# Routed experts of a two-layer Flamingo block: which operand is stationary, where the down weights come from, and how far ahead rows are gathered

## The chip, the cores and the metric

The program runs on one core of a Trainium2 chip. The time is the device time of one execution in microseconds (us), of which the median of several runs is taken. The engines are TensorE (PE, its weight loads PEld), VectorE (DVE), ScalarE (ACT), GpSimd (POOL) and SyncE (SP), which issues most transfers.

## What is computed

`x` is 8 tiles of 128 tokens by 256. Layer 0 adds a gated recurrent cross attention and then a gated mixture of experts; layer 1 adds a gated attention over the context and a gated feed-forward part with block-quantised weights and activations. The change touches the mixture of experts alone:

```python
idx, share = top 4 of 64 experts for each token      # router_w, softmax
for each expert e among them:
    h = silu(row @ wg[e]) * (row @ wu[e])            # row 256, wg and wu (64, 256, 64)
    y = y + share[e] * (h @ wd[e])                   # wd (64, 64, 256)
y = y + two shared experts(row)
x = x + tanh(g_ffn[0]) * y
```

## The kernel before, in words

All numbers are float32. The 1024 x 4 picks of tokens are sorted into 128 blocks of 64 rows (`S = 64`, `NBLK`). The first 64 blocks belong to fixed experts, block e to expert e (`NSTAT`); picks that do not fit there go to the other 64 blocks, whose expert is known only at run time, from the table `eid_row`. Four blocks are a "pair" (two tiles of 128 rows, each two blocks, `Q = 2`); there are `NP = 32` pairs, of which `NPS = 16` are fixed (0 to 15) and 16 are "chosen" (16 to 31). All up and gate weights (`moe_up`) and all down weights (`moe_dn`) are brought into SBUF.

Each pair goes through these steps, and each engine walks the pairs in one loop with an order written out by hand; semaphores tie the loops together:

- POOL gathers the pair's 256 rows from `h1_dram` by two indirect DMAs (L542) into `xg`, which has four buffers. Between them it rescales a chunk of the quantised weights of the last layer (L534).
- TensorE turns the rows (four transposes through the helper `turn`, L1214) into banks 0 and 1, and ScalarE copies them into `xgT` (L740). `xgT` has room for the two blocks of a tile apart, so that each can stand in a tile that is zero elsewhere; two memsets of VectorE (`clear`, L1001) provide the zeros.
- Up products: rows are stationary, weights move. In `up_fixed` (L1371) the two blocks of a tile use the left and right 64 columns of the array. In `up_chosen` (L1380) a tile with one block and zeros is stationary over all 128 columns, and the weights are picked by a register (`experts_of`, L337).
- ScalarE takes the silu of the gate half (L733), VectorE multiplies it by the up half into `hb` (L1078).
- Hidden turns: TensorE turns `hb` (two transposes), ScalarE copies the result into `hbT` (L754 for fixed, L756 and L757 for chosen pairs).
- Down products: four products of 64x64 stationary by 256 moving columns (L1398 fixed, L1401 chosen). For chosen pairs SP fetches the four experts' down weights a second time from DRAM into `dnS` (L399), two pairs ahead.
- ScalarE copies the result into `ysb` (L746), and SP stores it to `ys_dram` (L418).

In TensorE's loop step k does: up products of pair k, row turns of pair k + 1, down products of pair k - 2, hidden turns of pair k - 1. VectorE also quantises the last layer's weights in halves (`weight_half`), one half for each fixed pair and two for each chosen pair. Behind the routed stage TensorE turns these weights (`mx_turns`, L1214, with fill products `keep_warm`, L1444, between), POOL gathers the experts' results for each token (L566), and VectorE adds them up and normalises (L1095, L1152); then the attention of layer 1 begins.

Before the stage, at 84 us, stand the router's products (L1309, 64 moving columns) and those of the shared experts (L1237 and L1224, 256 moving columns).

## Time and profile before

| what | value |
|---|---|
| median of 3 runs | 512.68 us (511.4 to 513.83) |
| time of the profiled execution | 514.03 us |
| its span, first to last instruction | 512.3 us |
| mean granted TensorE clock | 0.92 of full speed |
| TensorE busy | 406.5 us, 79% |
| VectorE, GpSimd, ScalarE busy | 351.4, 247.5, 181.4 us |
| routed stage, first up product to first turn of the last layer's weights | 158.7 to 290.4 us |
| first up product of a chosen pair | 214.6 us |

The profile is one execution as the hardware profiler recorded it. Times within it are us from the start of the span. A line such as L1380 is a line of the kernel's source. The span is shorter than the time of the same execution, because the latter also has what lies before the first and behind the last instruction.

### The profile page before, as it was taken

The page shows a single profiled execution, that of the slowest core. Times are in us where ns is not written, and L with a number is a line of the kernel's source. Part 1 is how long each engine was busy: PE and PEld are TensorE (multiplying, and loading weights), DVE is VectorE, ACT ScalarE, POOL GpSimd, SP SyncE. Part 2 cuts the span into 40 slices and gives each one's busy share as a digit, 9 for nine tenths or more (in the row PEclk, how much of TensorE's full clock was granted, in tenths as well). Part 3 has the DMA queues.
Part 4 walks back from the last instruction along what each step waited for, and adds up shares of the span by engine and source line. Part 5 has one row for each costly group of instructions (what it writes and reads, how often), then busy time and mean ns, then how long its engine had stood idle before and what let it go on. Part 6 is the DMA issues. An engine that isn't in the chain of part 4 may idle for free.

```text
span 512.3 us, 8514 instructions
## 1 busy us (share of the span) xinstructions
PE 406.5 (79%) x2839; PEld 289.6 (57%) x2839; DVE 351.4 (69%) x840; ACT 181.4 (35%) x416; POOL 247.5 (48%) x347
## 2 busy tenths in 40 slices
PE   0476788778677899999699678768887899988884
PEld 0265666666446566677477456556665455555543
DVE  0568886656986455589577326857857699999992
ACT  0353465445301454444244242325354122222210
POOL 2356565423227577777441265866212245555451
PEclk9987798879959899999899699979997999999998
DMA  7999961112923597668954342433110000000000
GB/s 222 266 216 271 242 237 52 52 52 59 170 41 100 130 297 224 173 173 181 161 150 142 118 137 80 146 87 118 57 42 1 0 1 12 10 10 12 11 10 22
DMA packets 72314, 57.42 MB, mean 112 GB/s; under 512 B 38864, under 2 KB 64592, under 8 KB 72272
## 3 DMA queue, kind: packets, MB, share of 16 engines
q1 hardware_dynamic: 60880, 37.23, 27.9%
q0 software_dynamic: 4608, 12.59, 10.8%
q10 hardware_dynamic: 6784, 7.05, 4.1%
q8 instruction: 24, 0.39, 0.3%
q14 instruction: 18, 0.15, 0.1%
HBM read 42.18 MB, written 14.68 MB: 111 GB/s over the span
## 4 chain that ended last, share of the span: by engine, by line
PE 47%; issue 16%; DVE 15%; POOL 10%; ACT 3%; DMA 3%; ACTq 3%; another core or an unknown queue 2%; POOLq 0%; DVEq 0%
PE psum L1214 9%; PE psum L1380 6%; PE psum L1401 4%; PE psum L1237 3%; PE psum L1398 3%; POOL arena_dn L628 3%; PE psum L1371 3%; POOL mx_w L631 2%; PE psum L1224 2%; PE psum L1283 2%; DMA bias_bc<-_xattn_norm_k_img_w_dram 2%; PE psum L1229 2%; PE psum L1281 2%; PE psum L1470 2%
## 5 line engine op out<-in xcount | busy, mean ns | idle before, releaser
L542 POOL DMA_INDIRECT shared<-h_dram,tok_u x64 | 66.9, 1046 | 49.9 <-PE psum L1214 22.3
L1501 PE MATMUL psum<-arena_dn 128*128 128x512 f32 x128 | 57.1, 598 | 3.2 <-ACT arena_dn L785 3.2
L628 POOL TENSOR_TENSOR arena_dn<-arena_dn 128x512 f32<-128x512 f32 x16 | 20.3, 1271 | 45.6 <-DVE arena_dn L1047 45.6
L1501 PEld LDWEIGHTS psum<-arena_dn 128*128 128x128 f32 x128 | 23.7, 190 | 31.2 <-issue 26.3
L566 POOL DMA_INDIRECT arena_up<-ys_dram,slot_u x32 | 31.4, 981 | 14.1 <-issue 14.1
L1078 DVE TENSOR_TENSOR h1T<-psum,h1T 128x128 f32<-128x128 f32 x32 | 9.3, 292 | 40.0 <-ACT h1T L733 37.4
L1214 PE MATMUL psum<-ident,mx_w 128*128 128x128 f32 x128 | 23.3, 312 | 16.2 <-POOL mx_w L631 8.9
L1214 PE MATMUL psum<-ident,arena_dn 128*128 128x128 f32 x96 | 18.3, 310 | 21.8 <-DVE arena_dn L878 19.3
L1214 PE MATMUL psum<-ident,arena_up 128*128 128x128 f32 x144 | 25.0, 292 | 12.4 <-DVE arena_up L1105 2.9
L1214 PEld LDWEIGHTS psum<-ident,mx_w 128*128 128x128 f32 x128 | 16.8, 158 | 27.1 <-POOL mx_w L631 10.9
L1596 PE MATMUL psum<-arena_dn,mx_w 128*128 128x256 f32 x128 | 30.1, 390 | 0.4 <-ACT mx_w L795 0.3
L1214 PEld LDWEIGHTS psum<-ident,arena_dn 128*128 128x128 f32 x96 | 13.9, 163 | 26.4 <-issue 16.3
L1214 PEld LDWEIGHTS psum<-ident,arena_up 128*128 128x128 f32 x144 | 17.0, 147 | 20.2 <-DVE arena_up L1169 4.8
L1095 DVE SCALAR_TENSOR_TENSOR x_res<-arena_up,combs,x_res 128x256 f32<-128x256 f32 x32 | 16.5, 516 | 15.9 <-DMA arena_up<-ys_dram,slot_u 15.1
L746 ACT COPY stage<-psum 128x512 f32<-128x512 f32 x32 | 18.9, 591 | 24.0 <-PE psum L1401 14.9
L1401 PE MATMUL psum<-h1T 64*64 64x256 f32 x128 | 19.1, 419 | 10.3 <-issue 10.3
L733 ACT ACTIVATE h1T<-psum 128x128 f32<-128x128 f32 x32 | 8.9, 278 | 50.6 <-PE psum L1380 21.3
L1596 PEld LDWEIGHTS psum<-arena_dn,mx_w 128*128 128x128 f32 x128 | 24.5, 197 | 4.0 <-issue 0.8
L472 POOL TENSOR_SCALAR small<-mv 128x1 f32<-128x1 f32 (+2 forms) x26 | 6.1, 234 | 37.9 <-DVE mv L896 12.3
L790 ACT ACTIVATE arena_dn<-psum 128x512 f32<-128x512 f32 x16 | 9.6, 598 | 39.4 <-PE psum L1501 39.4
L475 POOL TENSOR_TENSOR rstd<-small,mhalf 128x1 f32<-128x1 f32 (+2 forms) x26 | 22.1, 850 | 2.2
L534 POOL TENSOR_TENSOR mx_w<-mx_w,wac 128x256 f32<-128x256 f32 x24 | 15.1, 627 | 13.2 <-DVE mx_w L1072 12.8
(226 smaller groups left out, 1065.4 us busy)
## 6 DMA issues: line engine op xcount, KB each, us to landing
ys_dram<-stage SPq DMA_DIRECT2D x32, 256.0 KB
arena_up<-in_L_ffn_wg_dram SPq DMA_DIRECT2D x8, 512.0 KB, 8.3
arena_up<-in_L_ffn_wu_dram SPq DMA_DIRECT2D x8, 512.0 KB, 7.4
h1T<-in_L_ffn_wd_dram SPq DMA_DIRECT2D x64, 64.0 KB
arena_dn<-in_L_ffn_wd_dram SPq DMA_DIRECT2D x3, 1024.0 KB, 11.5
va_dram<-stage ACTq DMA_DIRECT2D x8, 256.0 KB, 3.7
kT_dram<-stage ACTq DMA_DIRECT2D x8, 256.0 KB, 4.6
arena_up<-kT_dram SPq DMA_DIRECT2D x8, 256.0 KB, 2.7
```

Of the source, the lines that this page charges most:

```text
L475: pool.tensor_tensor(dst, temp, mhalf[:, 0:dst.shape[1]], ALU.pow).then_inc(sem(done), 1)
L542: pool.indirect_dma_start(out=xg[n % 4][:, b, :], out_offset=None, in_=h1_dram[:, :], in_offset=bass.IndirectOffsetOnAxis(ap=tok_u[:, 2 * ...
L566: pool.indirect_dma_start(out=yk[n % 3][k], out_offset=None, in_=ys_dram[:, :], in_offset=bass.IndirectOffsetOnAxis(ap=slot_u[:, n * K + k ...
L628: pool.tensor_tensor(haF[h], haF[h], heF[h], ALU.subtract).then_inc(sem("hint"), 1)
L746: act.copy(ysb[n % 2][:, :, :], bank[6 + n % 2][:, :].rearrange("p (b d) -> p b d", b=2))\
L1095: chain(dve.scalar_tensor_tensor(x_res[:, n, :], yk[n % 3][k], combs[:, n, k:k + 1], x_res[:, n, :], ALU.mult, ALU.add), "r")
L1214: return pe.transpose(dst, src, ident[0:k, 0:k])
L1237: ins = pe.matmul(sd_ps[t], hs[q % 2][:, f, at], sd_w[:, f, :], start=(f == 0), stop=(f == 3))
L1380: ins = pe.matmul(bank[2 + k % 2][:, 2 * F * b:2 * F * (b + 1)], xgT[k % 2][:, b, c, j, :], moe_up[:, c, bass.ds(experts[Q * b + j], 1), : ...
L1401: ins = pe.matmul(bank[6 + n % 2][at, b * D:(b + 1) * D], hbT[n % 2][j * F:(j + 1) * F, b, at], dnS[n % 2][j * F:(j + 1) * F, b, :], start ...
L1501: ins = pe.matmul(bank[2 * part + h][:, :], xTF[n % 2][:, c, :], mx_gu[:, c, lo:lo + HW], start=(c == 0), stop=(c == C - 1))
L1596: ins = pe.matmul(bank[4][:, 0:D], hTF[n % 2][:, i, :], mx_dn[:, i, :], start=(i == 0), stop=(i == 7))
```

## The change

- `up_fixed`: the weights of one expert (128 columns, 64 of up and 64 of gate) are stationary and the 64 turned rows of its block move. The result comes out with the hidden units on the partitions, so a fixed pair has no hidden turns: VectorE writes the hidden product as the stationary operand of `down_fixed`.
- `up_chosen`: a whole turned tile is stationary and each of its two experts' weights move over it, eight products of 128x128 by 128 columns into separate columns of one bank; rows of the other block give results that nobody reads. No zeros are needed, and the two memsets go.
- `down_chosen`: the turned hidden tile is stationary (64 rows by 128 columns), and each expert's down weights, picked in `moe_dn` by the registers that the up products used, move over it. SP's second fetch (`dn_load`, `dnS`) goes.
- Order: the down products follow their up products by one step in place of two, and for chosen pairs the hidden turns stand between up products and row turns.
- `xg` has six buffers in place of four, in the region `shared`; both `xgT` tiles lie in `stage`. POOL waits for the shared experts' last product before the fifth pair.
- The weights' quantisation takes three halves for every two pairs throughout, with four buffers of scales.
- ScalarE copies chosen results in two pieces, one for each half of the partitions.

```diff
 
-    return min(max(min(n, NPS - 1), 0) + 2 * max(n - NPS + 1, 0), 2 * NWC)
+    return min(max(3 * n // 2, 0), 2 * NWC)
...
-        xg = [take(2, D) for _ in range(4)]
-        xgT = [xgT1.rearrange("p (b c j n) -> p b c j n", b=2, c=C, j=Q), take(2, C, Q, P)]
+        XG = 6
+        xg = [take(2, D) for _ in range(XG)]
+        take = carver(stage)
+        xgT = [take(2, C, P) for _ in range(2)]
+        ysb = [take(2, D) for _ in range(2)]
         take = carver(h1T[:, :, :].rearrange("p c n -> p (c n)"))
-        sgb = [take(2, F) for _ in range(2)]
-        hb = [take(2, F) for _ in range(2)]
-        hbT = [take(2, P) for _ in range(2)]
-        dnS = [take(2, D) for _ in range(2)]
-
-        def own(tile):
-
-            return tile.rearrange("p x j (k n) -> p x (j k) n", n=S)[:, :, 0:Q * Q:Q + 1, :]
+        sgb = [take(4 * S) for _ in range(2)]
+        hb = [take(4 * S) for _ in range(2)]
+        hbT = [take(4 * S) for _ in range(2)]
...
-        wac = [sb(f"wac{i}", [P, WC // QB]) for i in range(2)]
+        wac = [sb(f"wac{i}", [P, WC // QB]) for i in range(4)]
...
-            def dn_load(n):
-                s = n % 2
-                if n >= NPS + 2:
-                    sp.wait_ge(sem("mo_y"), n - 1)
-                for x, v in enumerate(experts_of(mybir.EngineType.SP, n)):
-                    b, j = x // Q, x % Q
-                    sp.dma_start(dnS[s][j * F:(j + 1) * F, b, :], wd[bass.ds(v, 1)].rearrange("a f d -> f (a d)"))\
-                      .then_inc(sem(f"dn_in{s}"), 16)
-
-            sp.wait_ge(sem("eid"), 1)
             for n in range(NP):
-                if NPS <= n + 2 < NP:
-                    dn_load(n + 2)
...
-            for n in range(NP + 3):
+            for n in range(NP + 6):
                 if n < NP:
-                    reach(pool, sem("xgT_ps"), n - 3)
+                    if n == 4:
+                        pool.wait_ge(sem("sdown"), T)
+                    reach(pool, sem("xgT_ps"), n - XG + 1)
                     for b in range(2):
-                        pool.indirect_dma_start(out=xg[n % 4][:, b, :], out_offset=None, in_=h1_dram[:, :],
+                        pool.indirect_dma_start(out=xg[n % XG][:, b, :], out_offset=None, in_=h1_dram[:, :],
                                                 in_offset=bass.IndirectOffsetOnAxis(ap=tok_u[:, 2 * n + b:2 * n + b + 1], axis=0))\
-                            .then_inc(sem(f"xg{n % 4}"), 16)
-                due = min(weight_halves(n - 5) // 2, NWC)
+                            .then_inc(sem(f"xg{n % XG}"), 16)
+                due = weight_halves(n - 8) // 2
...
-            for k in range(-1, NP + 2):
+            for k in range(-1, NP + 1):
+                n = k - 1
+                if NPS <= n:
+                    act.wait_ge(sem("hT_ps"), n - NPS + 1)
+                    reach(act, sem("mo_y"), n - 1)
+                    act.copy(hbT[n % 2][0:F], bank[k % 2][0:F, 0:4 * S]).then_inc(sem("hbT"), 1)
                 if 0 <= k < NP:
                     act.wait_ge(sem("gu"), k + 1)
                     reach(act, sem("hb"), k - 1)
-                    act.activation(sgb[k % 2], bank[2 + k % 2][:, 0:4 * F].rearrange("p (b n f) -> p b n f", b=2, n=2)[:, :, 0, :],
-                                   ACT.Silu).then_inc(sem("sgb"), 1)
+                    if k < NPS:
+                        act.activation(sgb[k % 2][0:F], bank[2 + k % 2][F:2 * F, 0:4 * S], ACT.Silu).then_inc(sem("sgb"), 1)
+                    else:
+                        act.activation(sgb[k % 2].rearrange("p (x f) -> p x f", x=4),
+                                       bank[2 + k % 2].rearrange("p (x n f) -> p x n f", x=4, n=2)[:, :, 1, :],
+                                       ACT.Silu).then_inc(sem("sgb"), 1)
                 n = k + 1
                 if n < NP:
                     act.wait_ge(sem("xgT_ps"), n + 1)
                     reach(act, sem("gu"), n - 1)
-                    act.wait_ge(sem("cleared"), min(n + 1, 2))
-                    act.copy(own(xgT[n % 2].rearrange("p b c j n -> p (b c) j n")),
-                             bank[n % 2][:, :].rearrange("p (x j n) -> p x j n", j=Q, n=S)).then_inc(sem("xgT"), 1)
-                n = k - 2
+                    act.copy(xgT[n % 2], bank[n % 2][:, :].rearrange("p (b c n) -> p b c n", b=2, c=C)).then_inc(sem("xgT"), 1)
+                n = k - 1
                 if n >= 0:
+                    reach(act, sem(f"ys_out{n % 2}"), 16 * (n // 2))
                     act.wait_ge(sem("mo_y"), n + 1)
-                    reach(act, sem(f"ys_out{n % 2}"), 16 * (n // 2))
-                    act.copy(ysb[n % 2][:, :, :], bank[6 + n % 2][:, :].rearrange("p (b d) -> p b d", b=2))\
-                        .then_inc(sem("ysb"), 1)
-                n = k - 1
-                if 0 <= n < NP:
-                    act.wait_ge(sem("hT_ps"), n + 1)
-                    reach(act, sem("mo_y"), n - 1)
-                    turned = bank[4 + n % 2][0:F, 0:2 * P].rearrange("p (b n) -> p b n", b=2)
+                    at = 4 + 2 * (n % 2)
                     if n < NPS:
-                        act.copy(hbT[n % 2][0:F], turned).then_inc(sem("hbT"), 1)
+                        act.copy(ysb[n % 2], bank[at].rearrange("p (b d) -> p b d", b=2)).then_inc(sem("ysb"), 1)
                     else:
-                        act.copy(hbT[n % 2][0:F, :, 0:S], turned[:, :, 0:S])
-                        act.copy(hbT[n % 2][F:2 * F, :, S:P], turned[:, :, S:P]).then_inc(sem("hbT"), 1)
+                        act.copy(ysb[n % 2][0:S], psum[0:S, at:at + 2, 0:D])
+                        act.copy(ysb[n % 2][S:P], psum[S:P, at:at + 2, D:2 * D]).then_inc(sem("ysb"), 1)
...
-            def clear(tile):
-                dve.memset(tile.rearrange("p b c j n -> p (b c j n)"), 0.0).then_inc(sem("cleared"), 1)
-
...
-                    reach(dve, sem("w_deq"), n - 1)
+                    reach(dve, sem("w_deq"), n - 3)
...
-            for n in range(NP + 2):
+            for n in range(NP + 1):
                 if n < NP:
                     dve.wait_ge(sem("sgb"), n + 1)
-                    reach(dve, sem("hT_ps"), n - 1)
-                    dve.tensor_tensor(hb[n % 2], bank[2 + n % 2][:, 0:4 * F].rearrange("p (b n f) -> p b n f", b=2, n=2)[:, :, 1, :],
-                                      sgb[n % 2], ALU.mult).then_inc(sem("hb"), 1)
+                    if n < NPS + 2:
+                        reach(dve, sem("mo_y"), n - 1)
+                    else:
+                        dve.wait_ge(sem("hT_ps"), n - NPS - 1)
+                    if n < NPS:
+                        dve.tensor_tensor(hb[n % 2][0:F], bank[2 + n % 2][0:F, 0:4 * S], sgb[n % 2][0:F], ALU.mult)                            .then_inc(sem("hb"), 1)
+                    else:
+                        up3 = bank[2 + n % 2].rearrange("p (b x) -> p b x", b=2)
+                        sg3, h3 = (t[n % 2].rearrange("p (b x) -> p b x", b=2) for t in (sgb, hb))
+                        dve.tensor_tensor(h3[0:S, :, 0:F], up3[0:S, :, 0:F], sg3[0:S, :, 0:F], ALU.mult)
+                        dve.tensor_tensor(h3[S:P, :, 0:F], up3[S:P, :, 2 * F:3 * F], sg3[S:P, :, F:2 * F], ALU.mult)                            .then_inc(sem("hb"), 1)
...
+            chosen = {}
+
             def up_fixed(k):
+                for x in range(2 * Q):
+                    b, at = x // Q, slice(x % Q * S, x % Q * S + S)
+                    for c in range(C):
+                        ins = pe.matmul(bank[2 + k % 2][:, x * S:(x + 1) * S], moe_up[:, c, 2 * Q * k + x, :],
+                                        xgT[k % 2][:, b, c, at], start=(c == 0), stop=(c == C - 1))
+                ins.then_inc(sem("gu"), 1)
+
+            def up_chosen(k):
+                chosen[k] = experts_of(mybir.EngineType.PE, k)
+                for x in range(2 * Q):
+                    for c in range(C):
+                        ins = pe.matmul(bank[2 + k % 2][:, 2 * F * x:2 * F * (x + 1)], xgT[k % 2][:, x // Q, c, :],
+                                        moe_up[:, c, bass.ds(chosen[k][x], 1), :].rearrange("p a f -> p (a f)"),
+                                        start=(c == 0), stop=(c == C - 1))
+                ins.then_inc(sem("gu"), 1)
+
+            def hidden_turn(n):
+                pe.wait_ge(sem("hb"), n + 1)
+                reach(pe, sem("hbT"), n - NPS)
                 for b in range(2):
-                    for c in range(C):
-                        for j in range(Q):
-                            at = slice(j * S, (j + 1) * S)
-                            ins = pe.matmul(bank[2 + k % 2][at, 2 * F * b:2 * F * (b + 1)], xgT[k % 2][:, b, c, j, at],
-                                            moe_up[:, c, Q * (2 * k + b) + j, :], start=(c == 0), stop=(c == C - 1))
-                ins.then_inc(sem("gu"), 1)
-
-            def up_chosen(k):
-                experts = experts_of(mybir.EngineType.PE, k)
-                for b in range(2):
-                    for j in range(Q):
-                        for c in range(C):
-                            ins = pe.matmul(bank[2 + k % 2][:, 2 * F * b:2 * F * (b + 1)], xgT[k % 2][:, b, c, j, :],
-                                            moe_up[:, c, bass.ds(experts[Q * b + j], 1), :].rearrange("p a f -> p (a f)"),
-                                            start=(j == 0 and c == 0), stop=(j == Q - 1 and c == C - 1))
-                ins.then_inc(sem("gu"), 1)
-
-            def down(n):
-                pe.wait_ge(sem("hbT"), n + 1)
+                    ins = turn(bank[1 - n % 2][0:F, b * P:(b + 1) * P], hb[n % 2][:, 2 * b * F:(2 * b + 1) * F])
+                ins.then_inc(sem("hT_ps"), 1)
+
+            def down_fixed(n):
+                pe.wait_ge(sem("hb"), n + 1)
                 if 4 * n == 24:
                     pe.wait_ge(sem("moe_in4"), 16)
                 if 4 * n == E // 2:
                     pe.wait_ge(sem("moe_in2"), 16 * 2)
-                if n >= NPS:
-                    pe.wait_ge(sem(f"dn_in{n % 2}"), 64 * ((n - NPS) // 2 + 1))
                 reach(pe, sem("ysb"), n - 1)
-                for b in range(2):
-                    for j in range(Q):
-                        at = slice(j * S, (j + 1) * S)
-                        if n < NPS:
-                            ins = pe.matmul(bank[6 + n % 2][at, b * D:(b + 1) * D], hbT[n % 2][0:F, b, at],
-                                            moe_dn[:, Q * (2 * n + b) + j, :], start=True, stop=True)
-                        else:
-                            ins = pe.matmul(bank[6 + n % 2][at, b * D:(b + 1) * D], hbT[n % 2][j * F:(j + 1) * F, b, at],
-                                            dnS[n % 2][j * F:(j + 1) * F, b, :], start=True, stop=True)
+                for x in range(2 * Q):
+                    b, at = x // Q, slice(x % Q * S, x % Q * S + S)
+                    ins = pe.matmul(bank[4 + 2 * (n % 2)][at, b * D:(b + 1) * D], hb[n % 2][0:F, x * S:(x + 1) * S],
+                                    moe_dn[:, 2 * Q * n + x, :], start=True, stop=True)
                 ins.then_inc(sem("mo_y"), 1)
 
-            for k in range(-1, NP + 2):
+            def down_chosen(n):
+                pe.wait_ge(sem("hbT"), n - NPS + 1)
+                reach(pe, sem("ysb"), n - 1)
+                for x in range(2 * Q):
+                    b, j = x // Q, x % Q
+                    ins = pe.matmul(bank[4 + 2 * (n % 2) + b][:, j * D:(j + 1) * D], hbT[n % 2][0:F, b * P:(b + 1) * P],
+                                    moe_dn[:, bass.ds(chosen[n][x], 1), :].rearrange("p a d -> p (a d)"),
+                                    start=True, stop=True)
+                ins.then_inc(sem("mo_y"), 1)
+
+            for k in range(-1, NP + 1):
                 if 0 <= k < NP:
                     pe.wait_ge(sem("xgT"), k + 1)
                     reach(pe, sem("hb"), k - 1)
@@ -1412,30 +1412,26 @@
                         up_fixed(k)
                     else:
                         up_chosen(k)
+                if k > NPS:
+                    hidden_turn(k - 1)
                 n = k + 1
                 if n < NP:
-                    pe.wait_ge(sem(f"xg{n % 4}"), 32 * (n // 4 + 1))
+                    pe.wait_ge(sem(f"xg{n % XG}"), 32 * (n // XG + 1))
                     reach(pe, sem("xgT"), n - 1)
                     for b in range(2):
                         for c in range(C):
                             ins = turn(bank[n % 2][:, (2 * b + c) * P:(2 * b + c + 1) * P],
-                                       xg[n % 4][:, b, c * P:(c + 1) * P])
+                                       xg[n % XG][:, b, c * P:(c + 1) * P])
                     ins.then_inc(sem("xgT_ps"), 1)
                 if k < 1:
                     keep_warm(2, 3)
                 if k == 1:
                     pe.wait_ge(sem("xs"), T)
                     keep_warm(1, 7)
-                n = k - 2
-                if n >= 0:
-                    down(n)
-                n = k - 1
-                if 0 <= n < NP:
-                    pe.wait_ge(sem("hb"), n + 1)
-                    reach(pe, sem("hbT"), n - 1)
-                    for b in range(2):
-                        ins = turn(bank[4 + n % 2][0:F, b * P:(b + 1) * P], hb[n % 2][:, b, :])
-                    ins.then_inc(sem("hT_ps"), 1)
+                if 1 <= k <= NPS:
+                    down_fixed(k - 1)
+                elif k > NPS:
+                    down_chosen(k - 1)
```

## Rows read from the trace of the kernel before

**Rows 1.** Top of the page of the profile.

```profile
span 512.3 us, 8514 instructions
```

**Rows 2.** Busy time of each engine by stretch, PEclk, DMA share, GB/s.

```profile
158.70:168.80 10.10, 4.92 (x49) 3.68 (x48) 4.46 (x14) 1.66 (x5) 6.75 (x7) 1.00 0.31 92
168.80:176.40 7.60, 7.59 (x62) 4.89 (x64) 4.01 (x14) 3.11 (x8) 5.15 (x6) 0.78 0.44 111
176.40:214.60 38.20, 36.16 (x361) 22.58 (x361) 19.79 (x60) 18.80 (x50) 28.77 (x30) 1.00 0.84 234
214.60:240.80 26.20, 25.87 (x211) 20.27 (x212) 21.93 (x60) 11.53 (x32) 18.30 (x20) 1.00 0.71 180
240.80:258.20 17.40, 12.50 (x82) 10.33 (x80) 9.12 (x25) 5.09 (x14) 7.16 (x8) 0.80 0.86 156
...
280.70:290.40 9.70, 4.99 (x30) 2.21 (x29) 4.68 (x13) 2.86 (x8) 2.54 (x7) 0.73 0.44 136
```

**Rows 3.** Chain of waits over one fixed pair; start, us, what.

```profile
185.36 1.09 PE psum L1371 x16
186.46 0.58 PE psum L1214 x4
187.04 1.01 PE psum L1398 x8
188.05 0.34 PE psum L1214 x2
188.39 0.14 issue
```

**Rows 4.** Chain of waits over one chosen pair without a stall.

```profile
228.26 1.01 PE psum L1401 x8
229.27 0.34 PE psum L1214 x2
229.61 1.85 PE psum L1380 x16
231.46 0.44 PE psum L1214 x4
```

**Rows 5.** Chain of waits in the middle of the chosen pairs.

```profile
243.16 1.48 issue
...
248.28 3.43 issue
```

**Rows 6.** Chain of waits at the first two fixed pairs.

```profile
158.57 2.87 another core or an unknown queue
...
162.81 5.17 another core or an unknown queue
```

**Rows 7.** TensorE timeline of the router and shared experts; start, us, idle before.

```profile
84.05 0.66 PE L1309 MATMUL psum<-router_sb,h1T 128*128 128x64 f32 x4 [0.46 <-ACT h1T L714]
...
84.60 1.97 PE L1237 MATMUL psum<-shared,mx_w 128*128 128x256 f32 x8
86.41 1.03 PE L1224 MATMUL psum<-h1T,shared 128*128 128x256 f32 x4
```

**Rows 8.** Groups by line and form, 176 to 212 us.

```profile
L754 ACT COPY h1T<-psum 64x256 f32<-64x256 f32 x12 | 4.5, 373 | 0.0
```

**Rows 9.** All row gathers; duration ns min/median/max.

```profile
L542 POOL DMA_INDIRECT shared<-h_dram,tok_u x64: 943/991/1781, 150.1 to 263.6; - x64
```

**Rows 10.** Timeline of the start of the routed stage.

```profile
168.30 0.95 POOL L542 DMA_INDIRECT shared<-h_dram,tok_u  x1 [1.83 <-remote]
```

**Rows 11.** Chain of waits after the routed stage.

```profile
292.32 0.85 PE psum L1214 x4
...
296.52 0.44 PE psum L1214 x4
...
300.88 3.08 issue
```

**Rows 12.** VectorE timeline after the routed stage.

```profile
302.97 0.47 DVE L1152 TENSOR_SCALAR arena_up<-x_res,mv,rstd 128x256 f32<-128x256 f32 x1 [0.98 <-issue]
```

14 lines of the change are left out of this document (5 added, 9 removed).

## The prediction

> **What bounds the kernel now.** The span is 512.3 us [rows 1]; the profiled execution's own time was 514.03 us, the median of the runs shown 512.68. I add the change in us to the profile's time and carry it over to the median. I read, in this order: the stretches with each engine's busy time, to see where the diff acts and which engine is full there; the chain of waits in each stretch, to see what one pair of blocks costs; single forms, for prices that the routed stage does not show; and the stretch behind the stage, for what its end triggers.
>
> The diff acts between 158.7 and 290.4 us. TensorE is busy 36.16 of 38.20 us in the steady fixed stretch, 25.87 of 26.20 in the first chosen one, but 12.50 of 17.40 and 4.99 of 9.70 in later ones, where the granted clock is also 0.80 and 0.73 [rows 2]. So TensorE's own work bounds both kinds of pair while nothing stalls. A fixed pair is 1.09 (up) + 0.58 (row turns) + 1.01 (down) + 0.34 (hidden turns) + 0.14 of waiting = 3.16 us [rows 3]. A chosen pair is 1.01 + 0.34 + 1.85 + 0.44 = 3.64 us [rows 4]; sixteen would be 58 us, yet the chosen part takes 290.4 - 214.6 = 75.8. What is missing are holes in front of the down products, 1.48 and 3.43 us in one place [rows 5], and the half clock after them. In those holes the row turns have finished and the next instruction waits for its down weights, the only operand that is then still fetched.
>
> **Fixed pairs, up products.** Now the weights are stationary over all 128 columns and 64 rows of activations stream past. Eight products are sixteen loads of 128 columns. The router has just that form, 128x128 stationary and 64 moving: its four take 0.55 us from their start to that of the next group behind the small bf16 ones, 0.14 each with those counted in [rows 7]; the old chosen up, same loads with 128 moving, needs 1.85 for sixteen, 0.116 each [rows 4]. Neither gets below the load, so I take 1.86, against 1.09 now: the two 64-column halves that today run side by side [rows 3] are lost. The hidden turns go (0.34). So a new fixed pair is an old chosen pair without hidden turns: 1.85 + 0.44 + 1.01 = 3.30 us, +0.14 against 3.16. The Trainium skill ("TensorE: Matmul & The Clock Gate", section "LDWEIGHTS (loading the stationary operand)") puts a load by its columns alone, about 107 ns for 128; by that estimate the up products would be 1.71 and the pair 3.16, no change. The trace's 0.116 decides.
>
> Fourteen pairs (2 to 15) now take 214.6 - 168.8 = 45.8 us, the first at a clock of 0.78 [rows 2]. New: 14 x 3.30 = 46.2 plus some 1.5 for the same slow start, 47.7: **+1.9**. Bounds: -0.6, if the 0.17 of switching between half and whole array also goes (0.14 of it is the wait in [rows 3]); +4.7, if each pair pays 0.2 more, about the size of that wait and more.
>
> What else could bind there: ScalarE's copy of the turned rows lies under the down products, 1.01 us for about 0.6 (a copy of 64x256 takes 0.373 [rows 8]). VectorE is busy 19.79 of 38.20 us with one half of a weight chunk per pair; with one and a half it has about 2.4 us of work in 3.30. The hidden product becomes 64x256 and, priced like that copy, takes 0.4; two groups of products pass before it is read. POOL is busy 28.77 of 38.20 [rows 2], 2.4 a pair, and gets a quarter of a rescale more. All hidden; if POOL's cover were gone, a pair would cost POOL's 3.0, still below 3.30.
>
> **Start.** Two signals of TensorE reach ScalarE 2.87 and 5.17 us late, with no releaser shown [rows 6]. VectorE's two clears (removed) coincide with the slowest of the 64 gathers, 1.78 against a median of 0.99 [rows 9]; the second late signal comes at 162.81 + 5.17 = 167.98, and POOL, which waits for TensorE too, is idle for the 1.83 us before 168.30 [rows 10]. Removing the clears moves these gathers 0.8 to 1.6 us forward: I take **-0.8**, bounds 0 and -1.6.
>
> **Chosen pairs.** The down products lose their own fetch (four of 64 KB a pair, by the code), which fills the holes, but take the hidden activations as one 128-column stationary operand and the weights of one expert as 256 moving columns: eight instructions that fill the whole width. The shared expert's eight of 128x256 take 86.41 - 84.60 = 1.81 us [rows 7], against 1.01 now: +0.80 a pair. Up, row turns and hidden turns stay: 1.85 + 0.34 + 0.44 + 1.81 = 4.44 us. The hidden activations must be out before the down products: ScalarE's copy (0.373) starts after the hidden turn and is covered only by the row turns (0.44), so I add 0.06: 4.50. Register reads and address sums run in the sequencer while the array works, as for the up products now. Sum: pair 16 has no chosen down before it (3.3), fourteen at 4.50 (63.0), the last without row turns (4.0), and the tail of hidden turn, copy, down and two output copies (0.34 + 0.5 + 1.81 + 1.4 = 4.1): 74.4 us against 75.8, **-1.4**. Bounds: 4.44 gives -2.2; 4.70 (a wait of 0.2 for the copy) gives +1.4. Six rows ahead instead of four buys nothing here; no chain shows TensorE waiting for rows [rows 3, 4, 5]. SP loses four issues a pair, and only the stores stand behind them.
>
> **Behind the stage.** It starts at half clock: row turns of the weights take 0.85 us, later 0.44, and so do the fill products between them [rows 11]. Three rounds of 1.70 instead of 0.87 are 2.5 us. These turns gate the first query: the last follows after a hole of 3.08 us [rows 11], while the first normalised rows are ready at 302.97 + 0.47 = 303.44 [rows 12], 13.0 after the stage's end. Without holes in the chosen pairs TensorE ends the stage at full clock: **-2.5**; bounds 0 and -3.8 (the normalised rows become the gate).
>
> **Sum:** +1.9 - 0.8 - 1.4 - 2.5 = -2.8: 511.2 for the profiled execution, 509.9 for the median.
>
> **Rivals.**
> (a) The late signals follow the half-array up products (both are theirs) and vanish with them. Then the first two pairs take 1.85 + 0.44 + 0.9 and 1.85 + 0.44 + 0.4 + 1.01, 6.9 us in place of 10.1 [rows 2], and the slow clock behind them may go too: 3 to 4.5 less in place of 0.8, 506.5. Against it: the 3.08 us hole behind the stage looks alike with no half-array products there.
> (b) The late signals last as long as POOL gathers without a pause. Six ahead lets it issue two more pairs first, 4 x (0.99 + 0.3) = 5.2 us: +5.2 in place of -0.8, 515.9. For it: the coincidence above. Against it: later gathers run beside every pair and leave no such hole [rows 3, 4].
> (c) The other side: the copy of the hidden activations. Place: between hidden turn and down of fifteen chosen pairs. If signal, copy and signal take 0.8 instead of 0.5, each pair waits 0.35 more: +5.2, 515.1. It decides from a wait of about 0.35 us a pair, which would bring the sum to +2.5.
> (d) The time behind the stage does not follow TensorE (holes there remain and hide the clock): 0 in place of -2.5, 512.4.
> (e) The clock falls in the fixed stage, as the array streams 64 columns for each 128-column load. At half clock a pair costs nearly double, as [rows 11] shows for the turns: 3.3 more on half of fourteen pairs is +23, 533. [...] Against it: the fixed stretch holds 1.00 with 128 columns moving [rows 2], and its instructions would still follow without a gap.
>
> **How the numbers follow.** Forecast (sum) 0.46, (a) 0.17, (b) 0.11, (c) 0.11, (d) 0.11, (e) 0.04. The forecast's own range, with its bounds partly adding, is 507 to 514. The range over all: 504.5 to 516.5. 0.5% (about what a measurement of this kernel can tell from no change) is 2.6 us: faster holds (a) and somewhat over half of the forecast, 0.45; the same, the rest of it, most of (d) and a little of (b) and (c), 0.31; slower 0.24.
>
> **What would show it.** In the new profile: up products of fixed pairs at 1.8 to 1.9 us, down products of chosen pairs at 1.8 with less than 0.2 us in front of them, no fetch of down weights by SP, period 3.3 and 4.5, clock 1.00 from pair 3 to the turns of the weights. The prediction is wrong if the up products of fixed pairs fall below 1.5 us, if late signals change by more than 2 us, if the down products wait for the copy, or if the clock halves in the stage.

## The result, and the profile after

The changed kernel took 572.09 us (median of 4, 568.43 to 573.08) against 512.77 us for the kernel before (511.4 to 513.83): a ratio of 1.115, 95% interval 1.109 to 1.120. The forecast was 509.9, its range 504.5 to 516.5. The profiled execution took 572.28 us, its span is 570.5 us. On three other chips the same changed kernel takes 509 to 510 us; that is part of the explanation and comes with the experiments. Ratios with an interval are over the executions that the measurement counts as undisturbed, so they need not be the quotient of the medians beside them.

Busy time by stretch, PEclk, DMA share and GB/s, of the changed kernel; it answers to [rows 2]:

```profile
158.77:177.85 19.08, 10.49 (x55) 8.24 (x54) 4.68 (x15) 1.93 (x4) 10.38 (x11) 0.69 0.27 74
177.85:266.89 89.04, 89.04 (x394) 68.44 (x392) 34.43 (x98) 21.72 (x42) 32.20 (x37) 0.50 0.40 112
266.89:349.44 82.55, 77.64 (x487) 64.33 (x485) 46.97 (x136) 37.33 (x81) 28.30 (x38) 0.95 0.34 87
349.44:570.50 221.06, 186.27 (x1398) 125.81 (x1398) 162.52 (x328) 64.83 (x120) 103.43 (x128) 0.95 0.14 45
```

The stretches are the first two fixed pairs, the other fourteen, the chosen pairs, and what follows. The second one is most of the loss. The fourteen pairs take 89.04 us where the kernel before took 45.8; TensorE has no idle time in them, and its granted clock is 0.50, the lower of its two levels (1.2 GHz), throughout. The first stretch took 10.1 us before and takes 19.08. The chosen pairs take 82.55 instead of 75.8, the rest 221.06 instead of 512.3 - 290.4 = 221.9. With the 0.1 us by which the stage starts later and but for rounding, 9.0 + 43.2 + 6.8 - 0.8 makes the 58.2 us of 570.5 - 512.3.

The chain of waits of the changed kernel (start, us, what): the start of the stage, one fixed pair, one chosen pair, and the end of the stage.

```profile
158.69 9.85 another core or an unknown queue
...
184.28 3.60 PE psum L1362 x16
187.89 0.85 PE psum L1204 x4
188.74 1.90 PE psum L1391 x8
...
313.47 1.99 PE psum L1400 x8
315.46 1.98 PE psum L1370 x16
317.44 0.66 PE psum L1204 x6
318.09 0.10 issue
...
349.44 1.12 PE psum L1204 x4
```

Where [rows 6] had two waits for a late signal, 2.87 and 5.17 us, there is one of 9.85. TensorE stands idle for 8.59 us there, against 1.57 and 3.62 us in the kernel before. The clock falls in this hole, with TensorE at 0.00 busy (two stretches):

```profile
164.00:166.00 2.00, 0.00 (x0) 0.00 (x0) 0.00 (x0) 0.00 (x0) 1.65 (x2) 1.00 0.34 98
166.00:168.00 2.00, 0.00 (x0) 0.00 (x0) 0.00 (x0) 0.00 (x0) 1.19 (x2) 0.51 0.32 98
```

It comes back at about 272 us, some 5 us behind the first up products of a chosen pair, which have 128 moving columns. A fixed pair is 3.60 + 0.85 + 1.90 = 6.35 us, each part almost twice what it takes at full clock. A chosen pair is 1.99 + 1.98 + 0.66 + 0.10 = 4.73 us, at full clock, against 3.64 without a hole before [rows 4], and it has no hole beside the wait of 0.10 us. The trace counts a product of numbers in float32 as two instructions, so x16 are the eight up products and x8 the four down products of a pair. The turns behind the stage begin at half clock as in [rows 11].

### The profile page after: what moved, and what is told of

The parts are those of the page before. It is cut to its first block, busy times and chain, and to the rows that moved or that the text cites. A ratio compares the mean times of both kernels' runs of the same rounds, so it can differ in the third digit from the quotient of the medians.

```text
span 570.5 us, 8270 instructions
## 1 busy us (share of the span) xinstructions
PE 472.6 (83%) x2807; PEld 351.7 (62%) x2807; DVE 354.4 (62%) x854; ACT 188.2 (33%) x400; POOL 242.8 (43%) x347
## 4 chain that ended last, share of the span: by engine, by line
PE 56%; issue 16%; DVE 10%; POOL 8%; ACT 3%; DMA 3%; another core or an unknown queue 2%; ACTq 1%; POOLq 0%; DVEq 0%
PE psum L1362 9%; PE psum L1204 9%; PE psum L1370 6%; PE psum L1400 6%; PE psum L1391 5%; POOL arena_dn L614 3%; PE psum L1214 3%; PE psum L1219 2%; POOL mx_w L617 2%; PE psum L1440 2%; DMA mx_w<-in_L_xattn_o_w_dram 2%; PE psum L1555 2%; PE psum L1227 2%; PE psum L1273 1%
## 5 line engine op out<-in xcount | busy, mean ns | idle before, releaser
L528 POOL DMA_INDIRECT shared<-h_dram,tok_u x64 | 61.5, 960 | 101.3 <-PE psum L1204 74.2
L1362 PEld LDWEIGHTS psum<-stage,arena_up 128*128 128x128 f32 x256 | 54.2, 321 | 19.8 <-issue 10.6
L1362 PE MATMUL psum<-stage,arena_up 128*128 128x64 f32 x256 | 57.1, 415 | 8.6 <-ACT stage L734 8.6
L1064 DVE TENSOR_TENSOR h1T<-psum,h1T 64x256 f32<-64x256 f32 x16 | 6.7, 417 | 66.1 <-ACT h1T L725 66.1
L614 POOL TENSOR_TENSOR arena_dn<-arena_dn 128x512 f32<-128x512 f32 x16 | 20.3, 1269 | 45.8 <-DVE arena_dn L1029 45.8
L1400 PE MATMUL psum<-arena_dn,h1T 64*128 x128 | 32.3, 393 | 3.5 <-ACT h1T L720 2.0
L1370 PEld LDWEIGHTS psum<-arena_up,stage 128*128 128x128 f32 x256 | 31.4, 200 | 6.0 <-issue 6.0
L1370 PE MATMUL psum<-arena_up,stage 128*128 x256 | 34.6, 291 | 0.1
L1391 PE MATMUL psum<-arena_dn,h1T 64*64 64x256 f32 x128 | 30.8, 631 | 0.0
L1400 PEld LDWEIGHTS psum<-arena_dn,h1T 64*128 64x128 f32 x128 | 22.8, 187 | 10.1 <-issue 7.2
```

Of the source, the lines that this page charges most:

```text
L528: pool.indirect_dma_start(out=xg[n % XG][:, b, :], out_offset=None, in_=h1_dram[:, :], in_offset=bass.IndirectOffsetOnAxis(ap=tok_u[:, 2 * ...
L614: pool.tensor_tensor(haF[h], haF[h], heF[h], ALU.subtract).then_inc(sem("hint"), 1)
L1362: ins = pe.matmul(bank[2 + k % 2][:, x * S:(x + 1) * S], moe_up[:, c, 2 * Q * k + x, :], xgT[k % 2][:, b, c, at], start=(c == 0), stop=(c ...
L1370: ins = pe.matmul(bank[2 + k % 2][:, 2 * F * x:2 * F * (x + 1)], xgT[k % 2][:, x // Q, c, :], moe_up[:, c, bass.ds(chosen[k][x], 1), :].re ...
L1391: ins = pe.matmul(bank[4 + 2 * (n % 2)][at, b * D:(b + 1) * D], hb[n % 2][0:F, x * S:(x + 1) * S], moe_dn[:, 2 * Q * n + x, :], start=True ...
L1400: ins = pe.matmul(bank[4 + 2 * (n % 2) + b][:, j * D:(j + 1) * D], hbT[n % 2][0:F, b * P:(b + 1) * P], moe_dn[:, bass.ds(chosen[n][x], 1), ...
```

## The experiments

Two questions were open after the result: why the clock falls and stays down, and what the change costs without that. Theory A says that the narrow moving operand of the new up products (64 columns behind each 128-column load) holds the clock down by itself. Theory B says that the hole at the first pair throws it down, and a pair at half clock never brings it back. Theory C puts the loss on the chosen pairs. The kernels of one group of experiments ran on one chip, beside the kernel before; the changed kernel itself was not run again on the chip of the first four. Of each edit only the lines that matter are shown; where rows are stationary the hidden turns and their copy come back with them.

**Fixed pairs back to rows as the stationary operand**, chosen pairs and rows ahead as changed.

```diff
-                        ins = pe.matmul(bank[2 + k % 2][:, x * S:(x + 1) * S], moe_up[:, c, 2 * Q * k + x, :],
-                                        xgT[k % 2][:, b, c, at], start=(c == 0), stop=(c == C - 1))
+                            ins = pe.matmul(bank[2 + k % 2][at, 2 * F * b:2 * F * (b + 1)], xgT[k % 2][:, b, c, at],
+                                            moe_up[:, c, Q * (2 * k + b) + j, :], start=(c == 0), stop=(c == C - 1))
```

> The changed kernel with its fixed pairs put back to rows as stationary operand (two blocks side by side in 64 columns each, hidden turns, down products from the turned hidden tile); the chosen pairs stay as changed. Theory A (the narrow moving operand of the fixed up products, 64 columns for each 128-column load, holds the clock at half): the clock is 1.00 from about pair 3 to the end of the stage, a fixed pair takes 3.0 to 3.2 us, a chosen one 4.73 as in the changed kernel's full-clock part, and the time is 514 to 519 us. Theory B (the long hole at the first pair, 9.87 us of late signal, throws the clock down and a pair at half clock never earns it back): the clock falls here too if the hole is as long, and the time is over 550; if the hole is short as before, B says nothing. Theory C (the chosen pairs' change costs the time): 550 or more with the clock at 1.00.

Measured: 527.63 us against 514.14, ratio 1.028 (1.017 to 1.039). The late signal is there (chain):

```profile
158.70 10.77 another core or an unknown queue
```

but the clock comes back (stretches):

```profile
165.80:179.50 13.70, 9.20 (x54) 6.54 (x54) 3.81 (x12) 3.00 (x8) 4.76 (x6) 0.50 0.30 83
180.00:223.00 43.00, 37.75 (x396) 25.34 (x394) 31.48 (x94) 21.05 (x53) 32.84 (x36) 1.00 0.87 216
```

The form of the fixed pairs decides whether the clock returns. The time lies above what theory A gave, 514 to 519 us, since that left out the hole and the half clock behind it: the stage up to the first chosen pair takes 223.63 - 158.70 = 64.9 us, against 55.9 in the first profile of the kernel before. Theory B had the clock stay down and over 550 us.

**128 moving columns**: weights still stationary, all 128 rows of the block stream past, half of the products' columns unused.

```diff
-                        ins = pe.matmul(bank[2 + k % 2][:, x * S:(x + 1) * S], moe_up[:, c, 2 * Q * k + x, :],
-                                        xgT[k % 2][:, b, c, at], start=(c == 0), stop=(c == C - 1))
+                        ins = pe.matmul(bank[2 + k % 2][:, x * P:(x + 1) * P], moe_up[:, c, 2 * Q * k + x, :],
+                                        xgT[k % 2][:, x // Q, c, :], start=(c == 0), stop=(c == C - 1))
```

> The changed kernel with one edit in the fixed up products: all 128 turned rows of the tile stream past each expert's weights instead of the 64 of its block; the other 64 results are not read. Same number of loads and instructions. Theory A: the load-bound pair costs the same at full clock, 3.2 to 3.4 us, and the clock stays at 1.00 from about pair 3; time 514 to 522 us. Theory B: the first pair's hole comes again and the clock stays at half through the fixed pairs; 560 to 575 us.

Measured: 533.09 us (530.38 to 538.14), ratio 1.043 (1.032 to 1.054). Of TensorE's work only the moving width of the up products differs from the changed kernel (ScalarE and VectorE read as many results, from their new places). The hole is there, 10.76 us, and the clock returns at 173 us, 5 us behind it (stretches):

```profile
163.00:173.00 10.00, 5.05 (x22) 4.77 (x22) 3.31 (x10) 1.73 (x4) 3.20 (x5) 0.50 0.21 58
173.50:222.00 48.50, 48.50 (x398) 38.50 (x399) 34.12 (x96) 21.57 (x42) 33.87 (x38) 1.00 0.78 205
```

Doubling the streamed columns costs a pair 0.05 us at full clock (up products 1.98 against 1.93 us), and the kernel takes 39 us less than the changed one (572.09) did on its chip. On this chip it takes 40 us less than the kernel with narrow products and a fill that comes below (573.45). As put down before the run, theory B had the clock stay at half here too and gave 560 to 575 us. That is refuted. What is left of it is that narrow products at half clock don't bring the clock back, while wider ones do.

**Narrow products late**: pairs 0 to 7 with rows stationary, 8 to 15 as changed (`WS = set(range(8, 16))`).

> Pairs 0 to 7 with rows as stationary operand, pairs 8 to 15 with weights as stationary operand and 64 moving columns, chosen pairs as changed. Theory A: the clock is 1.00 up to about pair 8 and falls to half within a few pairs behind it; the pairs there take 6.36 us; it rises again in the first chosen pairs; time about 516 + 8 x 3.1 = 540 us. Theory B: the pairs enter at full clock without a hole, so it stays at 1.00, the pairs take 3.2 to 3.4 us, and the time is 515 to 521.

Measured: 530.21 us, one execution. This tests theory A. The clock is 0.50 only from 166 to 179.5 us. When the narrow products begin they find it at 1.00, and it stays there (stretches):

```profile
180.00:210.00 30.00, 27.73 (x262) 20.28 (x258) 22.55 (x63) 13.94 (x33) 21.89 (x24) 1.00 0.85 230
210.00:225.00 15.00, 14.66 (x122) 11.18 (x120) 11.91 (x32) 7.29 (x15) 11.15 (x12) 1.00 0.57 160
```

The chain over one narrow pair:

```profile
200.98 1.93 PE psum L1377 x16
202.91 0.44 PE psum L1219 x4
203.35 1.01 PE psum L1415 x8
```

It takes 1.93 + 0.44 + 1.01 = 3.38 us there. Theory A falls: as long as no wait interrupts them, narrow products keep either level that they find. The time is again above the 515 to 521 us expected, by the hole (9.40 us) and the half clock behind it, which came here too.

**A fill product of 256 columns in each fixed step**, in the changed kernel.

```diff
+                if k in range(2, 16):
+                    keep_warm(1, 7)
```

> The changed kernel with one fill product (128x128 stationary, 256 moving columns, result unread) in each of the fixed steps 2 to 15. At full clock it costs 0.43 us a pair, at half clock 0.86. Theory A leaves open whether this much streaming is enough: if it is, the clock is back at 1.00 and the time is 519 to 525 us; if not, 572 + 12 = 584. Theory B: no return, 584.

Measured: 573.45 us, one execution; the clock stays at 0.50 through the fixed pairs, and a pair takes 3.60 + 0.85 + 0.85 + 1.90 = 7.20 us. One product of 256 columns to eight narrow ones doesn't bring it back. The time is not the 584 us expected, though each pair pays 0.85 us for the fill, because the stage begins 6.2 us earlier (152.59) and its first two pairs take 13.2 us in place of 19.08. There is no hole of 10 us: TensorE waits twice, 1.95 and 2.28 us, and the clock is down from 159.6 us on, before the second wait. TensorE's timeline, a stretch, and the late signal as ScalarE's timeline shows it (`remote` stands there for a releaser that the profile doesn't have):

```profile
157.82 2.07 PE L1377 MATMUL psum<-stage,arena_up 128*128 128x64 f32 x16 [1.95 <-issue]
...
160.00:162.00 2.00, 2.00 (x8) 1.17 (x8) 0.00 (x0) 0.00 (x0) 1.44 (x2) 0.50 0.41 115
...
162.99 0.38 ACT L732 ACTIVATE h1T<-psum 64x256 f32<-64x256 f32 x1 [5.23 <-remote]
```

So the clock fell 2 us behind a wait of 1.95 us, without a long hole.

**Gathers never more than two pairs ahead**, in the changed kernel and then in the kernel before. This was to test rival (b) of the prediction, that the hole lasts as long as GpSimd issues gathers without pause. GpSimd's rescales of the weights also follow two or three pairs earlier in its loop.

```diff
-                    reach(pool, sem("xgT_ps"), n - XG + 1)
+                    reach(pool, sem("xgT_ps"), n - 1 if n > 2 else 0)
```

> The changed kernel, with one edit: GpSimd issues the gathers of a pair only when the turns of the pair before it are done, so that it is never more than two pairs ahead (the changed kernel issues 14 gathers without a pause before the first pair); the weights' rescales on GpSimd follow three pairs earlier in the loop. Theory P (the late signal at the first pair lasts as long as GpSimd issues gathers without pause, and the clock falls in that hole): the hole at the first pair is at most 3 us instead of 9.85, the granted clock stays at 1.00 (narrow products kept it there in the pairs 8 to 15 of the run with half of the pairs each way), fixed pairs take 3.3 to 3.6 us, and the time is 510 to 525 us. Theory Q (the clock falls at narrow products with any pause before them, or the hole does not depend on the gathers): the granted clock is 0.5 from the first pair on, pairs of 6.4 us, and the time is 560 to 575 us.

> The kernel before, with the same edit of the gathers alone (never more than two pairs ahead; it issues 12 without a pause). Theory P: the late signals at the first two pairs, 2.87 and 5.17 us, shrink to under 1.5 us each, and the kernel takes 3 to 8 us less than before (505 to 510 us). Theory Q (the holes do not depend on the gathers): the holes stay at 2.9 and 5.2 us, and the time is that of before within 2 us, or a few us more where a pair waits for its gather.

Measured, changed kernel: six executions between 515.36 and 550.48 us, median 541.18 against 500.38, ratio 1.034 (1.020 to 1.049). The mean granted clock is 0.933 and 0.918 in the two shortest, 515.36 and 521.9 us, and 0.872 to 0.891 in the other four. The trace is of one of these, 546.65 us. No hole stands at the first pair; but the gathers come late now, and the clock falls behind the wait for one. Chain, TensorE's timeline at the same place, then stretches:

```profile
172.99 6.27 DMA shared<-h_dram,tok_u
```

```profile
179.30 1.03 PE L1204 MATMUL psum<-ident,shared 128*128 128x128 f32 x4 [0.87 <-DMA shared<-h_dram,tok_u]
```

```profile
158.50:173.00 14.50, 14.50 (x117) 11.82 (x117) 9.21 (x29) 5.54 (x11) 7.33 (x8) 1.00 0.49 112
179.30:250.00 70.70, 70.70 (x312) 54.50 (x312) 27.64 (x74) 17.11 (x33) 26.44 (x30) 0.50 0.36 104
```

The gather takes 6.27 us to land, but most of that lies under work: TensorE waits for rows 0.50 us before 174.83 and 0.87 us before 179.30. Behind the second wait the clock is down, and narrow products keep it there to the end of the fixed pairs. That is what is left of theory B, with another and far shorter wait. Why only some executions fall isn't shown, and the median lies between what the two theories put down for this run gave (510 to 525 and 560 to 575 us).

Kernel before: 504.72 us against 500.38, ratio 1.014 (1.008 to 1.020), slower where theory P had 3 to 8 us less, as theory Q had it where pairs wait for their gathers; the chain has gathers of 6.65 and 5.53 us. Its clock falls as well, in a wait of 2.91 us that ends at 172.26, but is back at 1.00 by 178 us, and it stays there over later waits of 0.45, 0.77 and 1.33 us. TensorE's timeline at the last of these, and the stretch behind it:

```profile
201.57 0.66 PE L1214 MATMUL psum<-ident,shared 128*128 128x128 f32 x4 [1.33 <-DMA shared<-h_dram,tok_u]
...
202.00:204.00 2.00, 2.00 (x22) 1.11 (x21) 0.39 (x1) 1.30 (x3) 1.20 (x2) 1.00 0.06 22
```

In these two profiles, then, the narrow form loses the clock at a wait of 0.87 us and the form of before keeps it over 1.33. Rows need more than two pairs of lead. What neither run could show is the effect on the late signal, since no kernel on this chip had one, not even the one with four pairs ahead below, which doesn't pause its gathers.

**Four pairs ahead instead of six** (`XG = 4`), twice, and the changed kernel and the kernel before again.

> The changed kernel with four pairs of rows ahead instead of six, as the kernel before had (10 gathers without a pause before the first pair instead of 14). Theory P with the length of the burst as the only thing that counts: the last gather of the burst ends some 4 us earlier, the hole at the first pair is 4 to 6 us; if that is still enough for the clock to fall, the stage runs at 0.5 and the time is 560 to 570 us; if not, it is 510 to 525 us. Theory Q (the hole has another source): hole of 9 to 10 us and 568 to 574 us.

> The changed kernel itself, beside the kernel before and four rows ahead on one chip. Theory S (the late signals at the first pairs come and go with the chip, and the rows ahead have no part in it): if this chip shows the hole, the time is 568 to 574 us with the clock at 0.5 from 166 us; if it shows none, the clock stays at 1.00 and the time is 508 to 515 us, that of four rows ahead within 2 us. Theory R (six rows ahead themselves bring the hole or the fall of the clock): 555 us or more here while four rows ahead takes 508 to 515 us on the same chip.

> The kernel before itself, for a profile on this chip. Theory S: its late signals at the first two pairs (2.87 and 5.17 us in the first profile) are gone if the time is near 500 us, and are there if it is near 513 us. The holes in the chosen pairs (4.74 us for a pair on the average, against 3.64 for one without a hole) are there in either case, since they follow the fetches of the down weights.

> The changed kernel with four pairs of rows ahead instead of six, now timed. Without a hole at the first pair 508 to 515 us, 1.5 to 2.5% over the kernel before; if its clock falls in some executions as it did with the paused gathers, its times spread over 510 to 560 us.

Four ahead: 510.74 us, one execution, on the chip of the paused gathers. On a third chip: four ahead 511.52 (510.46 to 513.99), ratio 1.023 (1.015 to 1.031); **the changed kernel itself 509.7 (505.08 to 512.83) against 499.49 (496.11 to 503.47), ratio 1.0135 (1.003 to 1.024; the medians give 1.020)**; the kernel before, profiled, 501.01. Stretches of the changed kernel on that chip:

```profile
155.70:210.40 54.70, 54.34 (x447) 43.26 (x447) 39.80 (x112) 23.94 (x47) 43.54 (x47) 1.00 0.77 207
210.40:291.91 81.51, 76.58 (x485) 63.16 (x485) 47.94 (x138) 37.10 (x81) 28.75 (x38) 0.97 0.37 88
291.91:508.62 216.71, 182.93 (x1398) 124.43 (x1398) 162.08 (x328) 64.78 (x120) 103.29 (x128) 0.96 0.15 46
```

and of the kernel before:

```profile
157.36:207.02 49.66, 47.99 (x469) 30.99 (x469) 27.64 (x87) 25.54 (x60) 38.85 (x42) 0.97 0.78 213
207.02:282.04 75.02, 61.53 (x495) 47.69 (x495) 53.02 (x148) 31.06 (x84) 34.03 (x44) 0.97 0.68 164
282.04:499.28 217.24, 183.52 (x1398) 124.82 (x1398) 162.42 (x328) 64.74 (x120) 103.42 (x128) 0.96 0.15 46
```

No signal is late in either, the clock is 1.00 through all narrow pairs, and by these two profiles the change costs 9.3 us: -1.7 by an earlier start, +5.0 in the fixed pairs, +6.5 in the chosen ones, -0.5 behind. The executions of four and six ahead overlap; no gain from the two more pairs is seen. And in the first profile of four ahead GpSimd issues sixteen gathers with no pause over 0.35 us, 147.70 to 168.33 us, while no signal is late: a long run of gathers isn't enough to make the hole.

**The burst cut**, to try rival (b) once more: the gathers of pair 3 and on wait for the turns of pair 1, and go six ahead later. Theory P is rival (b), the run of gathers makes the signal late; theory S says that it comes with the chip, whatever GpSimd does.

```diff
-                    reach(pool, sem("xgT_ps"), n - XG + 1)
+                    reach(pool, sem("xgT_ps"), 2 if n == 3 else n - XG + 1)
```

> The changed kernel, six pairs ahead as it is, with the first burst of gathers cut in two: those of pair 3 and on wait for the turns of pair 1, so that GpSimd issues nothing while the first up products' signal is due. Beside the changed kernel on the same chip. If that chip shows the late signal for the changed kernel: theory P (the burst makes it) gives a hole under 3 us here, a clock of 1.00 and 508 to 530 us against 568 or more; theory S (the signal is late on some chips whatever GpSimd does) gives the same hole of 8 to 10 us and the same 565 to 575 us. If it shows none: both take 505 to 515 us, and the two theories are not told apart.

> The changed kernel itself, on this chip: 568 to 574 us with the hole of 9 to 10 us at the first pair and the clock at 0.5 from 166 us, or 505 to 515 us without one, with the clock at 1.00.

> The changed kernel with the first burst of gathers cut in two, on one more chip: under theory P no hole over 3 us and 505 to 530 us whatever the changed kernel shows there; under theory S the same hole and the same time as the changed kernel, within 5 us.

> The changed kernel itself on the same chip: 568 to 574 us with the late signal and the clock at 0.5 from 166 us, or 505 to 515 us without one.

> The kernel before on the same chip: near 513 us with late signals of 2.9 and 5.2 us at its first two pairs if the changed kernel has its own there, near 500 us with none if not.

Measured on a fourth chip: 508.72 cut (ratio 1.033, 1.024 to 1.041), 509.43 as changed (one execution), 496.69 before; on a fifth, one execution each, 508.41, 509.6, and two of the kernel before, 503.13 and 496.68. No signal was late in any, so cutting the run could show nothing; that the changed kernel, with its whole run of gathers, had none on three chips only says that the run isn't enough. Over all profiles the late signals go with the chip, as the line of shares on the profile's page says. Of the changed kernel on its first chip, and on the third one:

```profile
PE 56%; issue 16%; DVE 10%; POOL 8%; ACT 3%; DMA 3%; another core or an unknown queue 2%; ACTq 1%; POOLq 0%; DVEq 0%
```

```profile
PE 52%; DVE 17%; issue 13%; POOL 12%; ACT 2%; DMA 2%; ACTq 1%; POOLq 0%; DVEq 0%
```

The entry "another core or an unknown queue" stands in the first two profiles and in the four of the chip of the first experiments, with 2 or 3% in five of these six. In that of the fill products it is 0% and lies outside the stage, but the timeline has the late signals there too (5.23 us above). It stands in none of the fourteen taken on the four other chips, whatever the kernel, and none of them has a wait for `remote` at the start of the stage.

**The chosen pairs' down products in half-array tiles again**, from fetched weights. First with the products one pair behind, three buffers and paused gathers; then two pairs behind, as in the kernel before, and gathers unpaused. Fixed pairs have rows stationary in both.

```diff
-                    ins = pe.matmul(bank[4 + 2 * (n % 2) + b][:, j * D:(j + 1) * D], hbT[n % 2][0:F, b * P:(b + 1) * P],
-                                    moe_dn[:, bass.ds(chosen[n][x], 1), :].rearrange("p a d -> p (a d)"),
+                    ins = pe.matmul(bank[4 + 2 * (n % 2)][j * S:(j + 1) * S, b * D:(b + 1) * D],
+                                    hbT[n % 2][j * F:(j + 1) * F, b * P + j * S:b * P + j * S + S],
+                                    dnS[n % 3][j * F:(j + 1) * F, b, :], start=True, stop=True)
```

> A version that takes from each side what the runs so far favour: rows stationary in the fixed pairs with the turns of the products beside the next pair's up products, the chosen pairs' up products as changed, their down products again in half-array tiles from fetched down weights (three buffers, fetched two pairs ahead), rows four pairs ahead with the gathers never more than two pairs ahead of the turns. If the down products by register (1.99 us for 8) are what makes the chosen pair 4.73 us, it is 3.7 to 3.9 us here with no hole, and with a short entry hole (theory P) the time is 496 to 505 us. If fetching the down weights holds the pair up, there are holes at the waits for them, the chosen pair is 4.4 us or more, and the time is 508 to 518 us. Under theory Q the entry hole stays at 8 to 10 us, which adds 6 to 10 us to either.

> The combined version with its down products two pairs behind the up products, as in the kernel before, and gathers without a pause: rows stationary in all fixed pairs, eight separate up products in the chosen ones, half-array down products from fetched down weights with three buffers instead of two. If the two buffers were what made the holes of the kernel before in its chosen pairs, and the short chain through the copy of the turned products what kept the last version at 4.24 us, a chosen pair takes 3.7 to 3.9 us, and the time is 12 to 16 us under the kernel before. If the DMA queues set the pace there (768 KB for each pair), a chosen pair stays at 4.2 us or more, and the time is within 4 to 8 us under the kernel before.

> The version with three buffers on another chip: 0.98 to 0.993 of the kernel before. If this chip has the late signals, its wide products bring the clock back within some 4 us and the ratio is the same; its hole then costs it what it costs the kernel before, 5 to 12 us.

Measured, one pair behind: 504.47 against 500.38, ratio 1.004 (0.998 to 1.010), which is no difference; a chosen pair 4.24 us, since the down products wait for the copy of the turned ones. Two pairs behind: **494.97 against 499.49 us, ratio 0.988 (0.982 to 0.993)**, and on the fourth chip 494.18 against 496.69, 0.991 (0.984 to 0.997). It is about 1% faster than the kernel before and so beats both kernels. It gained less than the 12 to 16 us that were expected if the buffers were the limit, and comes nearest to the other case put down (4 to 8 us, the transfers set the pace). Its stretches, then its chain:

```profile
156.34:203.81 47.47, 46.48 (x470) 30.13 (x469) 37.80 (x110) 25.00 (x60) 38.41 (x43) 1.00 0.80 218
203.81:265.90 62.09, 57.39 (x452) 45.01 (x451) 41.44 (x119) 29.07 (x74) 31.28 (x36) 0.97 0.77 178
```

```profile
232.03 0.44 PE psum L1229 x4
232.46 1.01 PE psum L1452 x8
233.47 0.34 PE psum L1229 x2
233.81 1.96 PE psum L1404 x16
...
242.69 13.31 DMA ys_dram<-stage
```

A chosen pair is 0.44 + 1.01 + 0.34 + 1.96 = 3.75 us while the transfers keep up, but they don't to the end: a store to `ys_dram` takes 13.31 us, and the fifteen pairs average 62.09 / 15 = 4.14. With the third buffer the first holes come later (0.56 us at 236.21, against 0.57 us at 224.21 in the kernel before on that chip), but they come. That fits the DMA share of 0.77 there, against 0.37 in the chosen pairs of the changed kernel, which fetches no down weights. The medians differ by 4.5 us, the two profiles by 499.3 - 490.0 = 9.3, so the shares are rough: 1.0 by an earlier start, 49.66 - 47.47 = 2.2 in the fixed pairs, 75.02 - 70.61 = 4.4 in the chosen ones with their tail, 1.7 behind. The third buffer was not tried alone, so which of this is its gain isn't shown.

## Why the prediction was wrong

**The clock, rival (e).** This is the step that failed: the fourteen fixed pairs were worked out as 47.7 us at full clock and took 89.04 at 0.50, which is 41.3 of the 43.2 us more there, of 58.2 in all. The prediction took the full clock in every term of the fixed pairs but 1.5 us, and priced its fall at half of the fourteen pairs with a chance of 0.04. The reason given against it, that the instructions "would still follow without a gap", held from pair 2 on (89.04 of 89.04 us busy) and did not help. The other reason, the 1.00 of the fixed stretch in [rows 2], was read from products of 128 moving columns, and the width was just what the change halved. The gap that mattered was at the first pair, and it stood in [rows 6] already. The kernel before has the same fall there, 0.78 as the mean of the first 7.60 us [rows 2], and gets over it, since its products bring the clock back. What had to be asked is what brings the clock back, and whether the change takes that away. The wide and the late experiment show it: narrow products without a wait were enough to keep the clock at 1.00, and not to lift it from 0.50. Rival (e) named the width, but not the hole, as the cause; its half of fourteen pairs was a guess. The Trainium skill ("TensorE: Matmul & The Clock Gate", section "HAM oscillation — how this bites in real kernels") describes a kernel with little work between its waits, whose clock falls in each wait and oscillates. The trace agrees that a wait throws the clock down. It shows no oscillation: here 89 us without a wait pass at 0.50, and on another chip 54.70 us at 1.00.

**The start, -0.8.** Right on a chip without late signals only in sign: the stage starts 1.7 us earlier, but its first two pairs take 162.60 - 155.70 = 6.9 us instead of 162.19 - 157.36 = 4.8. That 6.9 is what rival (a) had worked out. On the first chip the start cost +9.0. Rival (b) has the right direction for 1.8 of it (9.85 against 2.87 + 5.17 = 8.04), but its cause isn't shown: sixteen gathers without a pause brought no late signal. TensorE's idle time grew by 3.4 us (8.59 against 1.57 + 3.62), the second pair at half clock costs 3.5 more than at full (3.67 against 1.93 us for its up products, and so on), and the new form costs the 2.1 of the third chip. Removing the clears didn't shorten the hole.

**Fixed pairs, +1.9.** Right where the clock holds. Worked out were 47.7 us for the fourteen pairs; on the third chip they take 210.40 - 162.60 = 47.8. The kernel before needs 207.02 - 162.19 = 44.8 there, 1.0 less than in the first profile, so the term is +3.0. Up products were taken as 1.86 us and are 1.81 behind the fill products of the first two pairs, but 1.93 behind the half-array ones. The lower bound of -0.6 took off a switching time of 0.17 us that the 3.30 doesn't show as a part, and 1.9 - 14 x 0.17 is -0.5; nothing hangs on it.

**Chosen pairs, -1.4.** Wrong in size and sign: +6.8, and +6.5 on the third chip, beyond the bound of +1.4. Fourteen pairs were put at 4.50 and take 4.73: the down products 1.99 instead of 1.81, the up products 1.98 instead of 1.85, the turns 0.66 instead of 0.78, the wait 0.10 instead of 0.06; +3.2 in all. The shared expert's eight instructions of 128x256 in [rows 7] were too low a price for these eight; that their neighbours of another form make the difference is likely, but no run shows it. Pair 16 was put at 3.3 us and takes 3.65. The last pair and the tail were put at 8.1 us and take 291.91 - 280.23 = 11.7, +3.6, from the start of the last up products (280.23 in the timeline, 280.30 in the chain). In the tail the last down products run at half clock and cost 3.79 us (third chip, chain):

```profile
280.30 1.98 PE psum L1370 x16
...
283.04 2.00 PE psum L1400 x8
...
286.31 0.38 ACT h1T L720
286.69 0.13 issue
286.82 3.79 PE psum L1400 x8
...
291.91 1.11 PE psum L1204 x4
```

The mechanism was right: no down product waits for a fetch, and rival (c) didn't come, as the copy is covered but for 0.10 us. But sixteen dearer pairs cost 6.5 us more than the holes had.

**Behind the stage, -2.5.** It is -0.8, and -0.5 on the third chip, inside its bounds and near rival (d). The turns still start at half clock (1.11 us the first): the waits of the tail, 0.53 and 0.58 us for copies, come last, whatever the pairs before them do.

Without the late signal the terms would have had to read -1.7 + 2.1 + 3.0 + 6.5 - 0.5 = +9.4, against the -2.8 forecast. So also there the prediction is wrong, by its chosen pairs first: their down products and their tail were priced too low.

**Open.** What makes the signals late was not settled. They came on the chip of the first pair of profiles and on that of the first experiments (whether these are two chips or one isn't known), and on none of the four others. They are signals that TensorE sends and ScalarE waits for, as in [rows 6]. Whether a cut of the gathers shortens the hole on a chip that has one was not tried, for want of such a chip in the later runs. That the clock falls in the hole and returns under wider products, not under the narrow ones, is shown by the first three experiments and the changed kernel's own chosen pairs; that a short wait will do, by the fill products and the paused gathers, each in one profile. How short a wait the narrow products bear was not measured.

## What to carry to other kernels

When a change makes the products narrower, don't ask only whether they keep the clock: look in the profile for the places where it falls now (a hole, a start) and for the work that brings it back, since that may be what the change removes. Then one short wait can cost the whole stretch behind it. Price a product, where you can, by a row in which it stands among the same neighbours, and price the tail of a stage by its own chain, wait by wait, at the clock that the holes of the tail leave. Where a fetch makes holes, weigh keeping the fetch and giving it a deeper buffer first; here the version that does so, with other changes, gained 1%, while the way around the fetch lost 1.4% (2% by the medians) on a chip without late signals.
